# Attention's end and the first steps of a quantised layer: where row maxima, weight scales and a maximum over partitions are made

## The reference, cut to what matters

```
x = x + attention(values=ctx, keys=ctx, query=layernorm(x), mask)     # 16 heads of 16 channels
x = x + quantised_mlp(layernorm(x))                                   # 256 -> 1024 -> 256
x = x + autocorrelation_attention(layernorm(x), ctx)
x = x + mixture_of_experts(layernorm(x))

quant_linear(x, w, b):
    s_in = max(max(x), 1e-8) / 255;  xq = clip(round(x / s_in), 0, 255) * s_in     # one scale for the whole tensor
    s_w  = max(max|w| per output row, 1e-8) / 127;  wq = clip(round(w / s_w), -128, 127) * s_w
    bq   = round(b / (s_in*s_w)) * (s_in*s_w)
    return xq @ wq.T + bq
quantised_mlp(x) = quant_linear(relu(quant_linear(x, w1, b1)), w2, b2)
```

## Time and profile before

| | us |
|---|---|
| median of three runs | 1350.01 (1347.45 to 1351.26) |
| the profiled execution | 1349.87 |
| its span, first to last instruction | 1348.1 |
| mean granted TensorE clock | 0.957 of 2.4 GHz |
| busy: TensorE, VectorE, ScalarE, GpSimd | 1171.1, 872.1, 597.2, 581.9 |
| last X add of the attention ends | 342.4 |
| quantised layer's block starts | 342.7 |
| maximum pass | 364.7 to 415.6 |
| autocorrelation starts | 485 |

### The profile page before, as it was taken

One profiled execution on the slowest core, in us unless ns is written; L12 is line 12 of the kernel. 1 busy time (PEld: TensorE's weight loads), 2 busy tenths in 40 slices (PEclk: granted clock), 3 DMA queues, 4 the chain that ended last, 5 costly groups with the idle time before them and its releaser, 6 DMA issues. The chain is left out here.

```text
span 1348.1 us, 28352 instructions
## 1 busy us (share of the span) xinstructions
PE 1171.1 (87%) x10137; PEld 892.3 (66%) x10148; DVE 872.1 (65%) x2546; ACT 597.2 (44%) x1065; POOL 581.9 (43%) x652
## 2 busy tenths in 40 slices
PE   0699999998477979977869999949999999999996
PEld 0244444444233658865759888838999999999995
DVE  4999999999687732237375685526666566666663
ACT  1387777775554722234056423304333333333331
POOL 6487777774340029965000006642333333333333
PEclk9999999999599989989879999969999999999998
DMA  9488888783320035610488033247888887888881
GB/s 279 85 173 166 167 165 173 166 179 101 127 63 1 0 102 164 221 75 1 125 216 170 2 127 118 103 139 237 252 253 252 252 261 244 245 247 245 256 254 43
DMA packets 183549, 217.30 MB, mean 161 GB/s; under 512 B 92944, under 2 KB 166288, under 8 KB 170912
## 3 DMA queue, kind: packets, MB, share of 16 engines
q1 hardware_dynamic: 169152, 199.19, 52.0%
q0 software_dynamic: 14304, 16.93, 5.9%
HBM read 144.70 MB, written 52.23 MB: 146 GB/s over the span
## 5 line engine op out<-in xcount | busy, mean ns | idle before, releaser
L1988 PE MATMUL banks<-moe_w,moe_hT 128*128 128x256 f16 x2640 | 296.9, 273 | 0.0
L1988 PEld LDWEIGHTS banks<-moe_w,moe_hT 128*128 128x128 f16 x2640 | 258.4, 98 | 30.0
L1899 ACT ACTIVATE moe_hf<-banks,moe_b 128x256 f32<-128x256 f32 x440 | 184.8, 471 | 169.7 <-PE banks L1975 169.7
L1843 POOL DMA_INDIRECT out_x<-moe_y,slot_owner x78 | 121.7, 1560 | 286.8 <-DVE moe_y L2221 243.3
L1975 PE MATMUL banks<-moe_rT,moe_w 128*128 128x256 f16 x1872 | 211.8, 273 | 0.0
L718 DVE CUSTOM_DVE_ANT_0 masked<-banks,mask_bias 128x256 f32<-128x256 f32 x512 | 185.5, 417 | 31.0 <-PE banks L541 28.8
L1975 PEld LDWEIGHTS banks<-moe_rT,moe_w 128*128 128x128 f16 x1872 | 183.8, 98 | 21.3
L2108 DVE TENSOR_TENSOR moe_hT<-moe_hf,moe_hT 128x512 f16<-128x512 f32 x220 | 153.8, 699 | 7.6
L470 ACT ACTIVATE probsT<-banks 128x1024 f32<-128x1024 f32 x128 | 130.8, 1022 | 51.0 <-PE banks L572 50.9
L541 PE MATMUL banks<-kT,qT 48*128 48x256 f16 x512 | 92.8, 286 | 46.6 <-DMA qT<-q_split 30.4
L1829 POOL DMA_INDIRECT slots_x<-moe_xn,pos x64 | 63.7, 995 | 154.4 <-DVE pos L2172 123.1
(11 more groups left out here) (310 smaller groups left out, 1802.2 us busy)
## 6 DMA issues: line engine op xcount, KB each, us to landing
moe_w<-moe_halves SPq DMA_DIRECT2D x80, 1024.0 KB, 5.0
moe_halves<-half_parts SPq DMA_DIRECT2D x18, 1024.0 KB, 6.5
slots_x<-empty_row SPq DMA_DIRECT2D x1, 10140.0 KB, 52.8
moe_rows<-slots_x SPq DMA_DIRECT2D x39, 260.0 KB, 5.8
half_rows<-in_L_ffn_Wfc SPq DMA_DIRECT2D x8, 1024.0 KB, 9.3
half_rows<-in_L_ffn_Wproj SPq DMA_DIRECT2D x8, 1024.0 KB, 8.5
moe_b<-in_L_ffn_bproj SPq DMA_DIRECT2D x39, 128.0 KB, 5.4
ctx_rows<-in_ctx SPq DMA_DIRECT2D x16, 256.0 KB, 3.0
```

The source lines that it names most:

```text
L1843: pool.indirect_dma_start(out=out_rows, out_offset=bass.IndirectOffsetOnAxis(ap=owner[:, s, t:t + 1], axis=0), in_=y[s % 2][:, t, :], in_o ...
L1899: ins = act.activation(hf[p][:, j, :], src, ACT.Gelu_apprx_tanh, bias=b1[buffer][:, j:j + 1], scale=1.0 / WSCALE)
L1988: ins = pe.matmul(OUT[p][:, t * D:(t + 1) * D], hT[p][:, x, j, t * P:(t + 1) * P], w2[buffer][:, w, j, :], start=(j == 0 and (w, x) == PAR ...
```

## The change

Six edits.

- `add` is done per tile: two instructions that add and, in the same instruction, take the maximum of the result over the row into `row_top`. The reduce in `see_rows` is gone. `see_rows` covers 30 of 32 tiles in the attention, in other steps.
- `see_weights` moves to step 0 of phase 15 and makes the scales and their reciprocals. ScalarE scales w2 in steps 3 and 4, w1 in steps 5, 6, 7 of phase 15 and step 1 of phase 16, and loads the table for the square root there. GpSimd rounds w2 at the end of its attention; VectorE rounds w1 in step 5 of phase 16. The rounded weights take the place of `k_split`.
- The last tile of the last batch goes back, and is projected, in `psum_o`, so `out_back(15, 1)` no longer waits for `normalise(15, 0)`. The last add of each tile waits for its own projection only.
- Both all-reduces go. VectorE puts the partial maximum on a diagonal, TensorE multiplies it by ones, so that all 128 values stand in each partition, and VectorE reduces them.
- The layer's first maximum is in TensorE's order behind the weight transposes and the spreading of sw2; the second stands behind the first two products of the second pass.
- GpSimd's eight pieces of cutting in the layer all start once the scale of X is there.

```diff
 def see_rows(v, g, X, lo, hi):
     for T in range(lo, hi):
         v.bn_stats(g.ln["stats"][:, T, :], X[:, T, :]).then_inc(g.mlp["rows_seen"], 1)
-    v.tensor_reduce(g.mlp["row_top"][:, lo:hi], X[:, lo:hi, :], AX.X, ALU.max).then_inc(g.mlp["rows_seen"], 1)
...
-        k_split = [sb(f"k_split{s}", [P, NQ, H, 4, DH], F16) for s in range(2)]
+        k_split = [w.bitcast(F16).rearrange("p (t h a e) -> p t h a e", t=NQ, h=H, a=4) for w in (g.mlp["w1q"], g.mlp["w2q"])]
...
+        def last_bank(b, t):
+            return psum_o if b == NB - 1 and t == 1 else psum_m
...
+            pool.wait_ge(g.mlp["scaled"], 1)
+            pool.tensor_scalar(g.mlp["w2q"][:], g.mlp["w2"][:].rearrange("p k f -> p (k f)"), ROUND, ROUND, ALU.add, ALU.subtract).then_inc(g.mlp["w2_rounded"], 1)
...
+                    if hp == 3 and B == NB - 1:
+                        scale_w2(0)
+                    if hp == 4 and B == NB - 1:
+                        scale_w2(1).then_inc(g.mlp["scaled"], 1)
+                    if hp >= 5 and B == NB - 1:
+                        scale_w1(2 * (hp - 5), 2 * (hp - 4))
+                    if hp == 1 and B == NB:
+                        scale_w1(6, 8).then_inc(g.mlp["scaled"], 1)
+                        act.preload_act_table(ACT.Sqrt)
                     if hp == 5 and real(B - 1):
                         copy_oT(B - 1)
...
                 if t == 0 and b >= 1:
-                    pe.wait_ge(s_xadd, b)
-                if t == 1:
+                    pe.wait_ge(s_xadd, NQ * b)
+                if t == 1 and b < NB - 1:
                     pe.wait_ge(s_on, NQ * b + 1)
...
             def add(b):
-                T = slice(NQ * b, NQ * (b + 1))
-                v.wait_ge(s_op, b + 1)
                 v.wait_ge(s_bias, b + 1)
-                v.tensor_tensor(X[:, T, :], X[:, T, :], psum_m.rearrange("p (t c) -> p t c", t=NQ), ALU.add).then_inc(s_xadd, 1)
+                for t in range(NQ):
+                    T = NQ * b + t
+                    v.wait_ge(s_op, NQ * b + (t + 1 if b == NB - 1 else NQ))
+                    v.tensor_tensor_reduce(X[:, T, :], X[:, T, :], last_bank(b, t)[:, t * D:(t + 1) * D], 1.0, -3e38, ALU.add, ALU.max,
+                                           g.mlp["row_top"][:, T:T + 1]).then_inc(s_xadd, 1)
...
-            AHEAD = {(NB - 1, 0): (0, 3), (NB - 1, 1): (3, 6), (NB - 1, 2): (6, 9), (NB - 1, 3): (9, 12), (NB - 1, 5): (12, 14),
-                     (NB - 1, 7): (14, 17), (NB, 3): (17, 20), (NB, 4): (20, 24)}
+            AHEAD = {(NB - 1, 2): (0, 2), (NB - 1, 3): (2, 6), (NB - 1, 4): (6, 8), (NB - 1, 5): (8, 12), (NB - 1, 6): (12, 15),
+                     (NB - 1, 7): (15, 18), (NB, 0): (18, 21), (NB, 1): (21, 25), (NB, 6): (25, 30)}
...
-                    if B == NB and hp == 0:
+                    if B == NB - 1 and hp == 0:
                         see_weights()
+                    if B == NB and hp == 5:
+                        round_w1()
...
...
-            for q in range(AHEAD):
-                cut_piece(pool, g.cut, first + q)
-            pool.wait_ge(m_pm, 1)
-            pool.partition_all_reduce(all_max[:], part_max[:], P, bass.bass_isa.ReduceOp.max).then_inc(m_am, 1)
-            pool.wait_ge(m_am, 1)
-            for q in range(AHEAD, PIECES * CUT_BESIDE_MLP):
+            pool.wait_ge(m_ab, 1)
+            for q in range(PIECES * CUT_BESIDE_MLP):
                 cut_piece(pool, g.cut, first + q)
-            pool.wait_ge(m_hp, 1)
-            pool.partition_all_reduce(h_all[:], h_part[:], P, bass.bass_isa.ReduceOp.max).then_inc(m_ha, 1)
...
+            pe.wait_ge(m_pm, 1)
+            pe.matmul(banks[2][:, 512:512 + P], ones[:], top_diag[:], start=True, stop=True).then_inc(m_am, 1)
...
                 values(c, jp)
+                if n == 1:
+                    pe.wait_ge(m_hp, 1)
+                    pe.matmul(banks[2][:, 512:512 + P], ones[:], top_diag[:], start=True, stop=True).then_inc(m_ha, 1)
...
-            v.tensor_reduce(part_max[:], row_top[:], AX.X, ALU.max).then_inc(m_pm, 1)
-            v.wait_ge(m_ws, 2)
-            v.tensor_scalar(w2q[:], w2[:], ROUND, ROUND, ALU.add, ALU.subtract).then_inc(m_wq, 1)
+            link(v.tensor_reduce(part_max[:], row_top[:], AX.X, ALU.max))
+            v.tensor_scalar(top_diag[:], ident[:], part_max[:, 0:1], None, ALU.mult).then_inc(m_pm, 1)
             v.wait_ge(m_am, 1)
+            link(v.tensor_reduce(all_max[:], banks[2][:, 512:512 + P], AX.X, ALU.max))
```

More of the change, by code:

```diff
@@ L483, in copy_out, with scale_w1, scale_w2 @@
                 act.activation(oT_raw[b % 2][:, quad, :], psum_o[:, 0:S], ACT.Copy).then_inc(s_ov, 1)
+            def scale_w1(lo, hi):
+                act.wait_ge(g.mlp["rows_seen"], g.mlp["scales_at"])
+                for j in range(lo, hi):
+                    ins = act.activation(g.mlp["w1"][:, j, :], g.mlp["w1"][:, j, :], ACT.Copy, scale=g.mlp["rw1"][:, j:j + 1])
+                return ins
+            def scale_w2(k):
+                act.wait_ge(g.mlp["rows_seen"], g.mlp["scales_at"])
+                return act.activation(g.mlp["w2"][:, k, :], g.mlp["w2"][:, k, :], ACT.Copy, scale=g.mlp["rw2"][:, k:k + 1])
             def copy_oT(b):
@@ new lines, in see_weights @@
+                v.tensor_reduce(sw2[:], g.mlp["w2"][:], AX.X, ALU.max, apply_absolute_value=True).then_inc(seen, 1)
+                v.wait_ge(seen, 2)
+                v.tensor_scalar(sw1[:], sw1[:], QEPS, 1 / 127.0, ALU.max, ALU.mult).then_inc(seen, 1)
+                v.tensor_scalar(sw2[:], sw2[:], QEPS, 1 / 127.0, ALU.max, ALU.mult).then_inc(seen, 1)
+                v.wait_ge(seen, 4)
+                v.reciprocal(g.mlp["rw1"][:], sw1[:]).then_inc(seen, 1)
+                v.reciprocal(g.mlp["rw2"][:], sw2[:]).then_inc(seen, 1)
@@ L757, in _, with round_w1 @@
+            def round_w1():
+                v.wait_ge(g.mlp["scaled"], 2)
+                v.tensor_scalar(g.mlp["w1q"][:], g.mlp["w1"][:].rearrange("p j c -> p (j c)"), ROUND, ROUND, ALU.add, ALU.subtract).then_inc(g.mlp["w1_rounded"], 1)
+            AHEAD = {(NB - 1, 2): (0, 2), (NB - 1, 3): (2, 6), (NB - 1, 4): (6, 8), (NB - 1, 5): (8, 12), (NB - 1, 6): (12, 15),
+                     (NB - 1, 7): (15, 18), (NB, 0): (18, 21), (NB, 1): (21, 25), (NB, 6): (25, 30)}
             g.mlp["ahead"] = max(hi for lo, hi in AHEAD.values())
-            g.mlp["seen"] = g.mlp["ahead"] + len(AHEAD) + 2
+            g.mlp["seen"] = g.mlp["ahead"] + g.mlp["scales_at"]
@@ L1117, in _ @@
             v.wait_ge(m_st, g.mlp["seen"])
[L1118 to L1129 removed]
+            see_rows(v, g, X, g.mlp["ahead"], NT)
+            v.wait_ge(m_st, g.mlp["seen"] + NT - g.mlp["ahead"])
             link(v.tensor_tensor(ln_a[:], stats[:, :, 1], stats[:, :, 4], ALU.subtract))
@@ L1136, in _ @@
             v.sem_inc(m_var, 1)
-            v.wait_ge(m_ws, 1)
-            v.tensor_scalar(w1q[:], w1[:], ROUND, ROUND, ALU.add, ALU.subtract).then_inc(m_wq, 1)
+            v.wait_ge(m_set, 4 + len(BIAS_ROWS))
+            for k in range(KC):
+                ins = v.tensor_scalar(sw2_diag[:, k, :], ident[:], sw2[:, k:k + 1], None, ALU.mult)
+            ins.then_inc(m_diag, 1)
             v.wait_ge(m_std, 1)
```

71 lines of the change are left out of this document (29 added, 42 removed).

## The result

The changed kernel takes 1339.5 us (median of 11 runs, 1334.4 to 1346.3); the kernel before, beside it, 1350.0 (11 runs). The ratio is 0.9912 with a 95% interval of 0.9889 to 0.9936, that is 11.9 us less, 8.6 to 15. Forecast were 5.8 less: the direction was right, but the gain is about twice the sum. Both are nearer to the second rival (1340.5) than to the sum.

What follows compares the result with a forecast made beforehand. Attention was taken to run at TensorE's pace, VectorE just behind, the layer's head as a serial chain on VectorE, ScalarE and GpSimd. Terms +1.2 + 0 - 8.9 + 1.0 + 1.0 = -5.7 gave 1344.2 us, range 1339 to 1348.5.

Steps and rivals of the forecast that it cites:

- second rival: TensorE's clock reaches its upper level earlier, from tail to maximum pass; 3 to 4 us more gained, 1340.5 us; chance 0.17.
- tail: Last weighing to last X add's end: 8.8 us instead of 12.2, with projections at the lower clock.
- head: Layer's start to first scaling of X: 8.1 us instead of 17.0, TensorE setting the maximum; -8.9 us.
- maximum pass: VectorE's first rounding of X now runs beside a GpSimd cut: +1.0 us (0 to 2).
- X add: Two adds with maximum per batch take 0.69 us instead of 0.60, unhidden in 13 attention phases: +1.2 us (0 to 10).
- Last phase: Attention's last phase: weight maxima and scalings queue ahead, two TensorE waits of about 2 us, last weighing ends +3.3 us later.
- First maximum on TensorE: In the layer's head: all-reduce on GpSimd would give the first maximum at 8.35 us, TensorE's product at 7.2.
- Second maximum: Before the second pass: TensorE's product stands behind eight matmuls, so the hidden scale comes +1.0 us later (0.5 to 1.5).
- Rounding beside the tail: W2's rounding on GpSimd (6.0 us) and W1's on VectorE (1.2 us), moved into the attention, are hidden.
- the attention's end: Sign: the attention ends within 1.5 us of before; ending 3 us later would make the prediction wrong.
- the clock of the pass: Sign: the prediction is wrong if TensorE's clock in the maximum pass differs from before.
- Rival 3: Gain given back in the attention's last phase, by an earlier clock fall or blocked rounding: +4 us, 1348.3 us; chance 0.24.

Runs made afterwards that it cites:

- run 1: Kernel before the change, with identity products whose result nobody reads put into TensorE's pauses in the tail and head; 1348.9 us, ratio 0.9992.
- run 11: Changed kernel with the last batch's last tile back in the shared PSUM area; 1337.6 us in its one execution.
- run 2: Changed kernel with 22 and 5 identity products around the transposes of X's first tiles, ahead of the maximum pass; 1338.7 us, ratio 0.9902.
- run 3: Changed kernel with both maxima over partitions back on GpSimd's all-reduce; 1345.9 us, ratio 0.997 to the kernel before.
- run 4: Changed kernel with only the second maximum over partitions back on GpSimd; 1337.4 us, ratio 0.9898 to the kernel before.
- run 7: Changed kernel with two of GpSimd's eight cutting pieces at the layer's start again, ahead of the scale; 1339.6 us.
- run 8: Changed kernel with 22 identity products in TensorE's pause early in the second pass; 1339.2 us, ratio 0.9913 to the kernel before.
- run 6: Changed kernel with the old 128x512 X add in batches 0 to 14 and row maxima by separate reduces; 1341.3 us, ratio 0.9925.
- run 5: Changed kernel with w1's maximum behind batch 13's X add on VectorE, and oT copied before w1's scalings on ScalarE; 1334.2 us, ratio 0.9868.
- run 10: Changed kernel with phase 15 reordered, second maximum on GpSimd, and identity products in TensorE's pauses from tail to second pass; 1333.1 us, ratio 0.987.
- run 9: Changed kernel with phase 15 reordered and the second maximum on GpSimd, no identity products; 1339.5 us, ratio 0.9921.

## Why the forecast was half of the gain

**The step that failed** is one assumption in three terms: TensorE's clock was taken to stand where it stood in the trace of the kernel before. The prediction says so in "the projections 3.78 at the lower clock" and "1.8 per 16 at this clock", and the term for the maximum pass has no clock in it. The runs showed the upper level in its place: projections of 1.99, 1.07 for 16 transposes, and 10.2 us of the pass at the lower level instead of 14.5. Split by the traces at either level, one trace for each number:

| stage | forecast | measured | work | clock | from |
|---|---|---|---|---|---|
| tail | -3.4 | -5.6 | -3.6 | -2.0 | 12.16, 10.20 (run 1), 6.59 |
| head | -8.9 | -10.0 | -9.1 | -0.9 | 17.30, 8.16 (run 11), 7.30 |
| maximum pass | +1.0 | -1.65 | -0.3 | -1.4 | 53.17 (run 1), 52.88 (run 2) |

The sum was -5.7. By stages, with the average of 2.2 for the adds in the attention, the measured one is +2.2 + 2.9 - 5.6 - 10.0 - 1.65 + 0.9 = -11.2, beside the 11.9 (8.6 to 15) of the runs. So 4.2 of the missing 5.5 us are clock, 1.3 the rounding, 0.9 other differences of work, and the adds take 1.0 away again. That the stages come so near to the runs is in part luck: of the six traces with the code of the change up to the tail's end (the change and runs 2, 3, 4, 7, 8) three lose another 1.3 to 1.6 us in the last phase, and the profiled one did not.

- **X add: price right, path mis-sized.** The pair repeats at 0.68. But +1.2 was a price on VectorE, while TensorE waited in more places, about 2.2 in all (run 6). The estimate worked out from the Trainium skill, "VectorE: DVE Perf Modes", section on the errata, was +2.0. That page's duration holds (0.42), but two adds overlap by 0.08, so its nearness to 2.2 does not confirm the way it was reached. Why 0.09 on VectorE becomes 0.17 a batch wasn't isolated.
- **Last phase: right.** Waits of 1.71 and 1.77 for two of about 2, and +2.9 for +3.3. Run 5 takes the first away, nearly halves the second and shortens the phase by 2.5, which names them right.
- **Tail: the work right, the clock wrong**, -3.6 for -3.4. The forecast's own 2 us for the upper level (run 1: 1.96) bring 8.8 to 6.8, and 6.59 was measured; with the clock falling at the projections run 5 has 8.27.
- **Head: the same.** "TensorE sets the maximum here" holds at the level that it was worked out for (run 11: 7.9 us from the block's start, forecast 8.1). At the upper level TensorE waited 1.17 for VectorE's diagonal, which came 5.2 us behind the block's start, forecast 5.45.
- **First maximum on TensorE: right in sign, 2.55 us for a forecast of about 1.2.** The rule that the Trainium skill has in "GPSIMD Engine Reference", Engine selection, to reduce over partitions on GpSimd, lost 2.55 at the first place and would have saved 0.90 at the second (runs 3, 4). The forecast put the difference down to TensorE being idle or busy. Run 3 shows another part: the first all-reduce started 3.4 us after its input was there. Whether it would win there too if started with that hidden wasn't tried.
- **Maximum pass: its rounding was mis-sized too.** The first rounding took 0.69, not 1.7: it began at 349.69, GpSimd's step at 349.72, and that one took longer instead (1.68, the next 1.15). At the upper level the pass is 0.3 shorter than before, not 1.0 longer.
- **Second maximum: right**, +0.90 for +1.0.
- **Rounding beside the tail, cuts in a row: right**, hidden, and run 7 shows the latter's worth.

Of the signs that the prediction gave, three spoke against it: the attention's end (2.4 us earlier, not within 1.5), the first rounding, and the clock of the pass, a difference of which it had called its refutation.

Rival 2 was the truth, and had 0.17. Its sizes were 2 in the tail, 1 in the transposes and about 3 in the pass; measured are 2.0, 0.9 and 2.7, of which last the change took half, so 4.2 for its "3 to 4". Which level the tail would have was open when it was predicted, and of the two the forecast took the one that was in the trace. Rival 3 exists too, only not in the profiled execution: of the eight traces with the two pauses (the change and runs 2, 3, 4, 6, 7, 8, 11) three (runs 3, 7, 8) have the clock down inside the last phase, which then took 19.5 to 19.8 instead of 18.2, and in four others of all traces (runs 5, 6, 9, 11) it fell between 334.8 and 337.3, which costs the tail 1.7 (8.27 and 8.22 of runs 5 and 9 against 6.59). It gives back 1.3 to 1.7 us, and 3.2 in run 7, where both stages are hit, not 4; it may be part of the spread of 12 us among the runs of the changed kernel.

Open: about 3 us of run 3's time, the low four runs of run 5, what moves the stages behind the layer by up to 6 us from one execution to the next, and what makes the clock fall early in one execution and not in another.

## What to carry to other kernels

Where a stage stands at the lower level of TensorE's clock, price the change at both levels: of the 11.2 us here 4.2 came through the clock (2.0 in the tail, 0.9 in the head, 1.4 in the pass). And follow what the clock does next: filling one pause moved the fall into the following pass and gave half back (run 1) or all of it (run 2); only with all pauses filled did stages and time keep it (run 10 against run 9). Work that left the serial chain of the head paid (9.1 us), even where what took it up (GpSimd, ScalarE between exponentials) is slower at it; but look for who stands behind it in the same queue, which cost 2.9 us here and was mendable, but for 0.4, by order alone. And before an engine is called slow at something, look at what it did between its input and its start: the first all-reduce took 0.38 of the 3.97 us.

## What of the hardware was unexpected

- The fall of the clock is not at a fixed place in the program: in traces with equal code ahead of it it came at 347.7 (the changed kernel), or already at 329.7 and 343.4 (run 3).
- A step of 0.18 us on 128x32 elements took 1.02 beside a cut on GpSimd (run 7); but which engine is held up is not told by who comes first. A rounding that began 0.03 us ahead of GpSimd's step took its 0.69, and the step 1.68; another began 0.61 behind GpSimd's step (362.42 and 361.81), and still took 0.68, the step 1.75 where others of its kind take 1.49.
- An add with the maximum over the row has the same start-to-start time (0.34) as the other fused operation on 128x256.
- VectorE waited 3.78 us for the first all-reduce over partitions (run 3) and 0.55 for the second, of the same shape (run 4). Either takes 0.38 itself. The first started 6.7 to 7.2 us after GpSimd's last other instruction in all three traces that have it, later than its input; the second had 18 us and more.
